# The setup of a fused two-layer attention and expert kernel: where rows are requested, how value weights are laid out, when zeros are written, and with which operations rows are normalised

## The reference

```
x = x + xattn(layernorm(x), ctx, ctx)        # 16 heads of 8; queries from x, keys and values from ctx
x = x + ffn(layernorm(x))                    # layer 0: 8 gated experts, top 2;  layer 1: 8 GELU experts, top 2
layernorm(x) = (x - mean(x)) / sqrt(var(x) + 1e-5)
Q = q @ Wq.T + bq;  K = k @ Wk.T + bk;  V = v @ Wv.T + bv
out = softmax(Q K^T / sqrt(8)) V @ Wo.T + bo
```

## Time and profile before

| | |
|---|---|
| three runs, us | 449.47, 455.15, 454.66; median 454.66 |
| profiled execution | span 452.7 us, first to last instruction; its time with what lies around the span is not recorded |
| mean granted TensorE clock | 0.883 of full |
| busy share of the span | PE 81%, DVE 78%, ACT 60%, POOL 57% |

### The profile page before, as it was taken

One profiled execution on the slowest core, in us unless ns is written; L12 is line 12 of the kernel. 1 busy time (PEld: TensorE's weight loads), 2 busy tenths in 40 slices (PEclk: granted clock), 3 DMA queues, 4 the chain that ended last, 5 costly groups with the idle time before them and its releaser, 6 DMA issues.

```text
span 452.7 us, 12731 instructions
## 1 busy us (share of the span) xinstructions
PE 365.6 (81%) x4450; PEld 261.0 (58%) x4450; DVE 351.1 (78%) x1007; ACT 272.5 (60%) x605; POOL 260.0 (57%) x342
## 2 busy tenths in 40 slices
PE   4586989887599999999987999878544699999900
PEld 3253566666346666566554677656433588889900
DVE  5785599998878786889777488988756899999806
ACT  4274688887356555565577688766422556767604
POOL 8860267787525559595950245486767426657640
PEclk9698599999589999999999599997755889999975
DMA  7267992000001111110014100000013123332137
GB/s 207 62 189 230 319 383 96 2 4 2 1 2 48 49 49 46 48 48 1 1 22 62 16 1 4 1 32 20 31 37 102 45 77 83 87 89 76 45 79 234
DMA packets 30837, 33.15 MB, mean 73 GB/s; under 512 B 3908, under 2 KB 22606, under 8 KB 30776
## 3 DMA queue, kind: packets, MB, share of 16 engines
q1 hardware_dynamic: 27692, 26.11, 20.2%
q0 software_dynamic: 2496, 5.18, 3.3%
q10 hardware_dynamic: 588, 1.05, 0.7%
HBM read 15.22 MB, written 15.01 MB: 67 GB/s over the span
## 4 chain that ended last, share of the span: by engine, by line
PE 51%; DVE 18%; POOL 13%; issue 8%; ACT 5%; DMA 3%; SPq 1%; POOLq 0%; DVEq 0%; ACTq 0%
PE ps L1348 10%; PE ps L1349 9%; PE ps L1350 9%; PE ps L1517 6%; PE ps L1438 4%; DVE area L957 3%; POOL sorted_rows L743 3%; PE ps L1412 2%; PE ps L1469 2%; POOL expert_sums L784 2%; POOL area L764 2%; ACT vals L426 1%; PE ps L1647 1%; POOL area L726 1%; DMA x_res<-in_x 1%
## 5 line engine op out<-in xcount | busy, mean ns | idle before, releaser
L764 POOL TENSOR_TENSOR area<-area 128x512 f16<-128x512 f32 x44 | 51.0, 1159 | 39.4 <-ACT area L554 39.3
L784 POOL DMA_INDIRECT expert_sums<-area x46 | 45.8, 997 | 35.3 <-ACT area L576 23.5
L1348 PE MATMUL ps<-area,w 128*128 128x512 f16 (+1 forms) x180 | 60.2, 335 | 6.5 <-DVE area L1264 5.0
L1348 PE MATMUL ps<-w,area 128*128 128x128 f16 (+1 forms) x360 | 64.4, 221 | 0.8 <-POOL area L764 0.8
L1349 PE MATMUL ps<-w,area 128*128 128x128 f16 (+1 forms) x360 | 64.3, 220 | 0.0
L1350 PE MATMUL ps<-w,area 128*128 128x128 f16 (+1 forms) x360 | 64.3, 220 | 0.0
L1349 PE MATMUL ps<-area,w 128*128 128x512 f16 (+1 forms) x180 | 60.1, 334 | 0.0
L1350 PE MATMUL ps<-area,w 128*128 128x512 f16 (+1 forms) x180 | 60.0, 333 | 0.0
L957 DVE TENSOR_REDUCE area<-ps 128x8 f32<-128x512 f32 x64 | 41.2, 686 | 17.7 <-PE ps L1517 16.9
L550 ACT ACTIVATE area<-ps 128x512 f32<-128x512 f32 x44 | 26.3, 597 | 36.4 <-PE ps L1350 35.8
L600 ACT ACTIVATE area<-ps,b_now 128x256 f32<-128x256 f32 x92 | 36.3, 475 | 15.2 <-PE ps L1350 15.1
(11 more groups left out here) (231 smaller groups left out, 1049.8 us busy)
## 6 DMA issues: line engine op xcount, KB each, us to landing
sorted_rows<-filler_rows SPq DMA_DIRECT2D x16, 528.0 KB, 6.1
w_stage<-in_L_ffn_W SPq DMA_DIRECT2D x8, 512.0 KB, 3.9
w<-sorted_rows SPq DMA_DIRECT2D x23, 132.0 KB
keys<-area SPq DMA_DIRECT2D x32, 48.0 KB
area<-in_ctx SPq DMA_DIRECT2D x4, 256.0 KB, 4.1
x_res<-in_x SPq DMA_DIRECT2D x4, 256.0 KB, 5.5
keys<-expert_sums SPq DMA_DIRECT2D x4, 256.0 KB, 5.5
keys<-expert_sums ACTq DMA_DIRECT2D x4, 256.0 KB, 6.1
```

Of the source, the lines that this page charges most:

```text
L764: nc.gpsimd.tensor_tensor(hid[:, n % 4, 1, :], gated[:, n % 4, :], hid[:, n % 4, 0, :], ALU.subtract).then_inc(q["lo"], 1)
L784: nc.gpsimd.indirect_dma_start(out=expert_sums, out_offset=bass.IndirectOffsetOnAxis(ap=to_row[:, j, h:h + 1], axis=0), in_=ys[j % OUTS][: ...
L1348: pe.matmul(dst, lhs[0], rhs[0], start=start, stop=False, **kw)
```

## The change

- SP no longer requests x. ACT requests group 0 of x as its first instruction, then the six bias rows as before, then groups 1 to 3.
- The value weights are written a second time (`wv_flat`, over the raw weights once those are transposed): for even heads with zeros in the columns of odd heads, and the other way round. ACT and DVE each get one more copy per layer for it, POOL two zero fills. `project_values` uses them, so that every column of the bank is either a value or zero, and high and low half of a block of values are one 128x512 operation each.
- POOL clears, before the first rows: `wv_flat` of layer 0 (after the weight transposes), only the ones column of `vals`, `bv_cols`, and group 0 of `keys` (2048 words). The rest (`later_zeros`: 6144 words of `keys`, `wv_flat` of layer 1 after the second weight transposes, `comb16`, `every16`, `b2_rows`) comes after the rows of all four groups and before attention. DVE no longer clears keys.
- Rows are (x + (-mean)) * rstd: a new POOL operation of one element per tile writes -mean, and the two row operations use add and multiply. The add of epsilon covers one element per tile rather than two.
- DVE's order: statistics of group 0 first; value bias columns and `constant_parts` move from group 0 to group 2, the cast of `minus_ones` from group 2 to group 3.

```diff
+            load_rows(0)
             act.wait_ge(s["ones"], 1)
...
+            for g in range(1, GROUPS):
+                load_rows(g)
...
+                act.wait_ge(s["wt_hi"], 4 * l + 3)
+                if l == 0:
+                    act.wait_ge(s["zero"], 2)
+                else:
+                    act.wait_ge(s["zero"], 7)
+                own, turned = value_weights(l, 0)
+                nc.scalar.activation(own, turned, ACT.Copy).then_inc(s["wt_hi"], 1)
...
-                for h2 in range(2):
-                    hi, lo, f = value_parts(j, h2)
-                    nc.scalar.activation(hi, f, ACT.Copy).then_inc(KV["v_hi"], 1)
+                hi, lo, f = value_parts(j)
+                nc.scalar.activation(hi, f, ACT.Copy).then_inc(KV["v_hi"], 1)
...
-            nc.gpsimd.memset(vals_flat[:, :].bitcast(F32), 0.0).then_inc(s["zero"], 1)
+            pool.wait_ge(s["wt_ps"], 1)
+            nc.gpsimd.memset(wv_flat[0].bitcast(F32), 0.0).then_inc(s["zero"], 1)
+            nc.gpsimd.memset(vals[:, :, :, :, :, :, HD:VW].rearrange("p i t b a h o -> p (i t b a h) o"), 0.0).then_inc(s["zero"], 1)
             nc.gpsimd.memset(bv_cols...)
-            nc.gpsimd.memset(keys[:, 1, :, :]...)
+            nc.gpsimd.memset(key_words[:, :, 0:GT // 2], 0.0).then_inc(s["zero"], 1)
+            def later_zeros():
+                nc.gpsimd.memset(key_words[:, :, GT // 2:tokens // 2], 0.0).then_inc(s["zero"], 1)
+                pool.wait_ge(s["wt_ps"], 2)
+                nc.gpsimd.memset(wv_flat[1].bitcast(F32), 0.0).then_inc(s["zero"], 1)
+                nc.gpsimd.memset(comb16...)
+                nc.gpsimd.memset(every16...)
+                nc.gpsimd.memset(b2_rows...)
...
-                nc.gpsimd.tensor_tensor(mv[:, bass.ds(t, width), :], mv_now[:, slot:slot + width, :], ..., ALU.add).then_inc(s["ag"], width)
+                nc.gpsimd.tensor_tensor(mv[:, bass.ds(t, width), 1:2], mv_now[:, slot:slot + width, 1:2], ..., ALU.add).then_inc(s["ag"], width)
+                nc.gpsimd.tensor_scalar(mv[:, bass.ds(t, width), 0:1], mv_now[:, slot:slot + width, 0:1], -1.0, 0.0, ALU.mult, ALU.add).then_inc(s["ng"], width)
                 pool.wait_ge(s["ag"], n + width)
...
                 nc.gpsimd.tensor_scalar(fx[...], x[:, t, :], mv[:, t, 0:1], rstd[:, t:t + 1],
-                                        ALU.subtract, ALU.mult).then_inc(KV["xh"], 1)
+                                        ALU.add, ALU.mult).then_inc(KV["xh"], 1)
...
             for g in range(GROUPS):
                 rstds(G * g, G, G * g, g % 2 * G)
                 queries_normalise(g)
+            later_zeros()
             attention(0)
...
+                dve.wait_ge(s["wt_lo"], 2 * l + 1)
+                if l == 0:
+                    dve.wait_ge(s["zero"], 2)
+                else:
+                    dve.wait_ge(s["zero"], 7)
+                own, turned = value_weights(l, 1)
+                nc.vector.tensor_copy(own, turned).then_inc(s["wt_lo"], 1)
...
+            group_statistics(0)
+            weights_low(0)
             context_low(0)
+            group_statistics(1)
             context_low(1)
...
-                if g == 0:
-                    value_bias_columns()
-                    constant_parts()
                 if g + 2 < GROUPS:
                     group_statistics(g + 2)
                     context_low(g + 2)
                 if g == 2:
+                    value_bias_columns()
+                    constant_parts()
+                if g == 3:
                     dve.wait_ge(s["ld_s"], 16 * (1 + 4 + 2 + 1))
                     nc.vector.tensor_copy(minus_ones[:, :], ones_raw).then_inc(s["ones"], 1)
...
+            sp.wait_ge(s["zero"], 6)
             place_keys(0, 1)
```

More of the change, by code:

```diff
@@ L43 @@
 VW = HD + 1
+WV_PAD = 2 * (P + HD)
 EXPERTS = 8
@@ L109, in build @@
         wT = sb("wT", [P, 2, 8, P], F16)
+        wv_flat = [w_raw[:, 4 * l:4 * l + 4, :].rearrange("p n d -> p (n d)")[:, 64:64 + 2 * WV_PAD // 2].bitcast(F16) for l in range(2)]
         col_raw = sb("col_raw", [P, P], F32)
@@ L291, in row_slot, with value_parts, value_weights @@
             return g if l else g % 2
-        def value_parts(j, h2):
-            rows = slice(64 * h2, 64 * h2 + 64)
-            f = ps[rows, 4 + j % 2, :].rearrange("p (s a h v) -> p s a h v", s=4, h=2, v=HD)[:, :, :, h2, :]
-            hi, lo = (vals[rows, c, 2 * j:2 * j + 2, :, :, h2, 0:HD].rearrange("p t b a v -> p (t b) a v") for c in range(2))
+        def value_parts(j):
+            f = ps[:, 4 + j % 2, :].rearrange("p (s v) -> p s v", v=HD)
+            hi, lo = (vals[:, c, 2 * j:2 * j + 2, :, :, :, 0:HD].rearrange("p t b a h v -> p (t b a h) v") for c in range(2))
             return hi, lo, f
+        def value_weights(l, i):
+            own = wv_flat[l][:, WV_PAD * i:WV_PAD * (i + 1)].rearrange("p (h c) -> p h c", h=2)[:, :, 0:P]
+            return own.rearrange("p h (a w) -> p h a w", a=PAIRS)[:, :, :, 0:HD], wT[:, i, 4 * l + 2, :].rearrange("p (a h v) -> p h a v", h=2, v=HD)
+        key_words = keys[:, :, :, :].rearrange("p i j k -> p (i j k)").bitcast(F32).rearrange("p (c k) -> p c k", c=2 * QUAD)
         block = ctx.enter_context(nc.Block())
@@ L314, in _ @@
                     (s["ld_c0"], s["ld_c1"], s["ld_c2"], s["ld_c3"])[g], 16)
-            for g in range(GROUPS):
-                sp.dma_start(x[:, G * g:G * (g + 1), :], x_dram[:, G * g:G * (g + 1), :]).then_inc((s["ld_x0"], s["ld_x1"], s["ld_x2"], s["ld_x3"])[g], 16)
             def place_keys(l, part):
@@ L339, in _ @@
             load_weights(1)
-            sp.wait_ge(s["zero"], 4)
-            sp.wait_ge(s["ones"], 5)
+            sp.wait_ge(s["zero"], 5)
             place_keys(0, 0)
@@ L625, in _ @@
             act.wait_ge(s["cols"], 1)
-            act.wait_ge(s["zero"], 3)
             def context_high(g):
@@ L751, in output_bias_rows @@
                 pool.wait_ge(s["b2"], 35)
-            pool.wait_ge(s["zero"], 4)
+            pool.wait_ge(s["zero"], 5)
             pool.wait_ge(s["ones"], 2)
@@ L874, in values_low @@
             def values_low(l, j):
-                for h2 in range(2):
-                    dve.wait_ge(KV["v_hi"], 4 * GROUPS * l + 2 * j + h2 + 1)
-                    hi, lo, f = value_parts(j, h2)
-                    nc.vector.tensor_tensor(lo, f, hi, ALU.subtract).then_inc(KV["v_lo"], 1)
+                dve.wait_ge(KV["v_hi"], 2 * GROUPS * l + j + 1)
+                hi, lo, f = value_parts(j)
+                nc.vector.tensor_tensor(lo, f, hi, ALU.subtract).then_inc(KV["v_lo"], 1)
             def queries_low(l, g):
@@ L1197, in normalise @@
                 dve.wait_ge(s["rs"], t + (1 + (2 * l + 1) * TILES))
+                dve.wait_ge(s["ng"], t + (1 + (2 * l + 1) * TILES))
                 nc.vector.tensor_scalar(rows_now[t // G][:, t % G * P:(t % G + 1) * P], x[:, t, :], mv[:, t, 0:1], rstd[:, t:t + 1],
-                                        ALU.subtract, ALU.mult).then_inc(F[l]["xd"], 1)
+                                        ALU.add, ALU.mult).then_inc(F[l]["xd"], 1)
             def rank(q, p):
@@ L1384, in project_values @@
             def project_values(l, j):
-                wv = W(l, "v")
-                positive_wait(pe, KV["v_lo"], 4 * GROUPS * l + 2 * j - 2)
+                wv = [[wv_flat[l][:, WV_PAD * i + P * h2:WV_PAD * i + P * h2 + P] for h2 in range(2)] for i in range(2)]
+                positive_wait(pe, KV["v_lo"], 2 * GROUPS * l + j - 1)
                 if l == 0 and j == 1:
@@ L1424, in attention @@
                 if l == 0:
-                    pe.wait_ge(s["ones"], 9)
+                    pe.wait_ge(s["ones"], 8)
                 pe.wait_ge(KV["q_lo"], GROUPS * (l + 1))
```

44 lines of the change are left out of this document (23 added, 21 removed).

## The result

The changed kernel takes 455.76 us (median of 18 runs, 452.14 the lowest) against 453.25 us for the kernel before (18 runs beside it): a ratio of 1.0082, 95% interval 1.0055 to 1.0109. Forecast were 444.5 us and a range of 440.5 to 451.5, so the time lies outside the range, on the wrong side.

A forecast was written before the change was run, and what follows sets the result against it. The setup was taken as a serial chain (x, rows of group 0, four loop turns), with DVE nearly the bound in attention 0. From 454.7, -7 - 1.5 - 0.8 - 0.9 = -10.2 gave 444.5 us, range 440.5 to 451.5.

The forecast's parts named there:

- Step 1: Setup start: x requested first, some 4.5 us sooner; early zeros take 3.0 us, POOL free at about 9.1, not 12.28.
- Step 2: Rows on POOL: row operation 0.43 instead of 0.80, negation 0.1; a group takes 3.3 instead of 4.63.
- first two rivals: On POOL: row operation costs what it did (0.80), 450.2, chance 0.30; negation costs a full scalar operation (0.80), 462.8, chance 0.07.
- Step 3: Setup loop: ACT's value pieces save 1.65, PE's clock not falling 2.0; last low half begins at 29.3, 8.1 earlier.
- Step 4: End of setup: later zeros fit, but the fill holds DVE in group 2, costing 1 (0 to 2); setup -7.
- Step 5: Behind the setup: attention 0 -1.5, end of layer-0 experts -0.8, layer 1 -0.9.
- third rival: Setup no shorter: DVE held by the long fill, PE's clock falling anyway, keys landing late; 451.5, chance 0.10.

The follow-up runs named there:

- zeros first: Changed kernel with the ones column, bv_cols and group 0 of keys filled before POOL waits for the weight transposes, value-weight zeros after: 451.84 us, ratio 0.999.
- the fill between two groups: Changed kernel with early zeros turned round and the long keys fill moved between rows of groups 1 and 2: 447.63 us, ratio 0.9922; again 446.52, 0.9872.
- cheap rows alone: Kernel before with only the negated mean and add and multiply for rows: 453.63 us, ratio 1.0015.
- both repairs: Changed kernel with early zeros turned round and value bias columns and constant_parts back in group 0 of DVE's loop: 448.23 us, ratio 0.9929.

## Why the prediction was wrong, by its steps

**Step 1, x and the first zeros: x right, the zeros mis-sized.** x of group 0 was there for the statistics at 4.07, as forecast (4 to 5). POOL's first add came at 13.42 where I had 9.1. I priced all early zeros by their words, 0.86 ns each, from a fill of adjacent words; the ones column is 1024 elements of two bytes that lie 18 bytes apart, and took 4.5 ns each: 4.62 instead of 0.9. I had no row of a strided fill, and put no bounds on its price. It cost 2.1 us of setup (zeros first), with DVE's held weight copy in it.

**Step 2, the row operation: right.** 0.45 to 0.47 against 0.43 forecast, the negation 0.19, a group on POOL 3.2 against 3.3. The first two rivals are out. The page cited against this (the Trainium skill, GPSIMD Engine Reference, Elementwise side-by-side cycle accounting) would, as I read its figure for a two-input add, have had add no cheaper than subtract; for the scalar form the runs show 0.45 against 0.78 with the same shapes.

**Step 3, the loop: right up to its last turn.** Turns of 4.51 against 4.5 forecast, and the clock at 1.00 in 12 to 22 us. From the rows of group 0 to the last low half it took 22.4 (16.68 to 39.08) where I had 16.9; without the 4.7 that the last turn has too much, 17.7. That the clock would fall behind a late wait of PE, as it did behind the hold, was in no term of the sum.

**Step 4, what is late next: this failed.** I saw that the long fill could hold DVE in group 2, put its ends at 0 and 2, and took 1. The cast was held 5.38, and the last turn of the loop took 4.7 more (9.18 against 4.51). My upper end took the hold to end at 28.2, because I had the fill at 22.9 to 28.2 (four groups of 3.3 behind 9.1 end at 22.3; I wrote 22.9), with DVE arriving late in it. In fact the two come there together: the rows of group 3 wait for statistics that stand in DVE's own loop, so the fill began at 27.23, when DVE came to its casts (27.11), and the hold had its full length. The early zeros are not the cause: with these turned round fill and cast came 2 us sooner, still 0.12 apart, and the cast took 5.38 again. What the place of the long fill cost is the step from that kernel to the one with the fill between two groups: the first cast at 34.37 rather than 41.16, 6.8 us. The two memsets of constant_parts, which I moved to group 2 at no cost, do cost nothing there without the hold: that kernel has them in group 2, and a last turn of 4.51. Setup: +2.3 instead of -7. The key copies had their room, as forecast: SP issued them from 36.87 and no later cast shows a wait for them.

**Step 5, the rest: attention 0 right, the later parts lost in the clock.** Attention 0 gained 1.3 (forecast 1.5), the layer-0 experts 0.4 (0.8), attention 1 1.6 (0.9). Together 3.3 against 3.2 forecast, but that is luck: 1.5 of the 1.6 stand in the first four steps of attention 1 (16.84 against 18.30), where the clock was 0.70 instead of 0.63, so that the gain forecast there is not shown. The last stage, which the change doesn't touch, took 1.9 more at 0.78 instead of 0.81.

The case that came is nearest to the third rival (the setup doesn't get shorter, 451.5), to which I gave 0.10 as something that takes three faults at once. One of its three, the hold, was nearly enough by itself: 6.8. The strided fill, which no rival has, brought 2.1. Together they are 8.9 of the 9.3 by which the first cast came later than the 33.9 of the sum (40.9 - 7). For the setup the rest of the mechanism was sound: with both faults mended the first cast is at 34.4 (forecast near 34). The forecast of the total was not reached even so. That kernel's ratios are 0.992 and 0.987, where 444.5 would have been 0.978; of its two profiled spans one is 11.2 shorter than before's and one 7.2.

Shown: the two faults, by kernels that mend them one by one and together. Shown for two executions of one kernel, on two chips: 3.0 of the 4.0 us between them stand in the first steps of either attention, where the clock was lower with the same work. Not shown: why one execution has the lower clock and another not, and whether the kernel with cheap rows alone gets it more often because its attention begins earlier. Its ten runs have mean clocks of 0.868 to 0.888; those of the kernel before beside it, but for one run of 594.79, 0.874 to 0.904. With both repairs attention begins as early, and its ten runs have 0.875 to 0.898.

## What to carry to other kernels

A fill that is taken off one engine's list has to be placed as carefully as a transfer: look at what the neighbour on DVE copies or casts in that stretch, not at whether the fill itself is on the path. Price a strided write by elements of its own kind, or bound it by the dearest element in the trace. And when a setup gain of 4 us doesn't show in the total, compare stage by stage with the granted clock beside it before doubting the gain.

## What was not expected of the hardware

- A POOL fill held DVE's copies and casts from and to SBUF, and cutting it into pieces did not help: 5.38 beside one fill, 5.67 beside eight that follow each other without a gap. Once a copy came through behind the second of three fills (3.60). Statistics, and operations that read PSUM, were not held (0.86, and 0.69 and 0.75, beside a fill of 5.22).
- A fill of 1024 two-byte elements 18 bytes apart takes POOL 4.57 to 4.63; 4608 adjacent words took 3.94 in the kernel with cheap rows alone. Clearing all of the tensor, as before the change, was the cheaper way.
- On POOL, (x + a) * b takes 0.45 where (x - a) * b takes 0.78, with the same shapes.
- Each of DVE's two memsets of 64x256 has 0.81 to 0.98 of idle "issue" ahead of it, in every kernel here.
